# Ternary feed-forward of a fused transformer kernel: TensorE takes the down-projection after the up-projection, VectorE the residual after the gating, and ScalarE normalises into two buffers ahead of the silu

## What is computed

```python
def act_quant(x):
    scale = 127.0 / jnp.clip(jnp.max(jnp.abs(x), axis=-1, keepdims=True), EPS)
    return jnp.clip(jnp.round(x * scale), -128.0, 127.0) / scale
def weight_quant(w):
    scale = 1.0 / jnp.clip(jnp.mean(jnp.abs(w)), EPS)
    return jnp.clip(jnp.round(w * scale), -1.0, 1.0) / scale
def bitlinear(x, w):
    return jnp.einsum('bsd,hd->bsh', act_quant(x), weight_quant(w))
h = jax.nn.silu(bitlinear(x, w1)) * bitlinear(x, w3)
return bitlinear(h, w2)

x = x + ffn(layernorm(x), w1, w2, w3)
```

## Time and profile before

| | |
|---|---|
| median of 3 runs | 1206.63 us (1204.51 to 1207.88) |
| the profiled execution's own time | 1209.69 us |
| its span, first to last instruction | 1207.9 us |
| mean granted TensorE clock | 0.958 of full speed |
| busy over the span: TensorE, VectorE, ScalarE, GpSimd | 90%, 69%, 39%, 37% |
| the stage `bit_ffn` in it | from 246 to 402 us |

### The profile page before, as it was taken

The page is one execution under the profiler, slowest core; times in us unless marked ns, Lnnn a source line. Parts: engine busy times, 40 slices in busy tenths (PEclk is TensorE's granted clock), DMA queues, the critical chain, the costliest instruction groups (busy, mean ns, idle before and its releaser), DMA issues. The chain is left out here.

```text
span 1207.9 us, 21482 instructions
## 1 busy us (share of the span) xinstructions
PE 1086.0 (90%) x5900; PEld 811.4 (67%) x5912; DVE 829.0 (69%) x1572; ACT 475.1 (39%) x1008; POOL 442.6 (37%) x355
## 2 busy tenths in 40 slices
PE   6999799958988698999899987999999999999997
PEld 5989676523443357989887765777777776777773
DVE  3548447848887546877896985767677676666656
ACT  1332134235553148888521162333333333333330
POOL 0000001135442110577662002655556566565520
PEclk8999999979999698999888998999999999999998
DMA  7334251323233368556065314879788798777659
GB/s 264 139 122 165 101 195 23 71 47 66 55 59 57 101 228 306 203 190 228 1 250 198 62 53 161 221 181 243 189 234 228 189 248 232 186 189 180 137 112 360
DMA packets 148189, 195.48 MB, mean 162 GB/s; under 512 B 62986, under 2 KB 80778, under 8 KB 148145
## 3 DMA queue, kind: packets, MB, share of 16 engines
q1 hardware_dynamic: 130512, 156.61, 40.8%
q0 software_dynamic: 17632, 38.32, 16.0%
HBM read 136.56 MB, written 50.34 MB: 155 GB/s over the span
## 5 line engine op out<-in xcount | busy, mean ns | idle before, releaser
L2362 POOL DMA_INDIRECT y_d<-tail,x_ox x78 | 163.1, 2092 | 136.2 <-ACT tail L2589 105.5
L1647 POOL DMA_INDIRECT e_rows<-r_d,x_ix x80 | 85.3, 1066 | 123.6 <-issue 106.2
L2434 PE MATMUL x_h<-x_w_hi,x_t_hi 128*128 x320 | 127.7, 399 | 2.2 <-DVE x_t_lo L2603 2.2
L2435 PE MATMUL x_h<-x_w_lo,x_t_hi 128*128 x320 | 127.5, 399 | 0.0
L2436 PE MATMUL x_h<-x_w_hi,x_t_lo 128*128 x320 | 127.4, 398 | 0.0
L2603 DVE TENSOR_TENSOR x_w_lo<-w,x_w_hi (+1 forms) x64 | 109.6, 1752 | 2.6 <-ACT x_w_hi L2560 2.6
L2551 ACT ACTIVATE e_rows<-x_h 128x256 f32<-128x256 f32 x80 | 30.8, 385 | 183.7 <-PE x_h L2436 172.6
L213 POOL TENSOR_TENSOR ln_rstd<-ln_ve,powers 128x2 f32<-128x2 f32 (+1 forms) x40 | 34.2, 856 | 172.1 <-DVE ln_ve L207 172.0
L2603 DVE TENSOR_TENSOR x_t_lo<-x_xb,x_t_hi 128x512 fp32r<-128x512 f32 x80 | 55.2, 692 | 42.5 <-ACT x_t_hi L2546 35.2
L1527 DVE SCALAR_TENSOR_TENSOR h_c<-h_qk,h_d 128x768 f32<-128x768 f32 x64 | 58.2, 951 | 26.0 <-PE h_qk L1421 9.4
L2453 PE MATMUL x_o<-x_w_hi,x_avt_hi 128*128 x160 | 71.6, 448 | 1.2 <-issue 1.0
(11 more groups left out here) (408 smaller groups left out, 2596.2 us busy)
## 6 DMA issues: line engine op xcount, KB each, us to landing
w<-in_L_ffn_w SPq DMA_DIRECT2D x32, 1024.0 KB
w<-in_L_ffn_w SPq DMA_DIRECT2D x32, 512.0 KB
h_negm<-negm_d SPq DMA_DIRECT2D x15, 1024.0 KB, 7.0
raw<-in_L_ffn_w SPq DMA_DIRECT2D x3, 2816.0 KB, 16.9
x_res<-in_x SPq DMA_DIRECT2D x8, 512.0 KB, 4.4
ctx_in<-in_ctx SPq DMA_DIRECT2D x8, 512.0 KB, 3.5
kt_d<-ct SPq DMA_DIRECT2D x8, 512.0 KB, 2.7
vc_d<-ctx_in SPq DMA_DIRECT2D x8, 512.0 KB, 2.7
```

The lines of the kernel that those rows point to most:

```text
L1647: nc.gpsimd.indirect_dma_start(out=xg[q][s], out_offset=None, in_=r_d, in_offset=bass.IndirectOffsetOnAxis(ap=ix[q][:, s:s + 1], axis=0), ...
L2362: nc.gpsimd.indirect_dma_start(out=y_d[s], out_offset=bass.IndirectOffsetOnAxis(ap=ox[q][:, s:s + 1], axis=0), in_=eo[q][s][:], in_offset= ...
L2434: nc.tensor.matmul(hbank[s], hi[:, k, :], w13p[0][:, at, k, :], start=k == 0, stop=False)
L2435: nc.tensor.matmul(hbank[s], hi[:, k, :], w13p[1][:, at, k, :], start=False, stop=False)
```

## The change

1. TensorE: in a round, u of tile t comes before `down(t-2)`.
2. VectorE: in a round, `hidden(t)` comes before `residual(t-2)`.
3. `f_xn` becomes two buffers, taken in turn. `normal(t)` therefore waits for `integers_x(t-2)` in place of `integers_x(t-1)` (the count of `xq_ready`).
4. ScalarE: `normal(t+2)` comes before `silu(t)`.
5. Before the first round: ScalarE does `normal(0)`, `normal(1)`, `grid_x(0)`, `grid_x(1)`; VectorE and GpSimd do `moments(1)` ahead of `spread_x(0)` and `integers_x(0)`.

```diff
-    xn = sbuf(st, "f_xn", [P, D])
+    xn = [sbuf(st, f"f_xn{u}", [P, D]) for u in range(2)]
...
         moments(0)
+        moments(1)
         integers_x(0, 0, 0)
-        moments(1)
         scales(0, 0)
...
             up(par, g_bank, w1t, g_ps)
+            after(pe, u_used, t)
+            if first:
+                pe.wait_ge(turned.w3_in, 16 * turned.turns["w3"])
+            up(par, u_bank, w3t, u_ps)
             if inner or t >= 2:
                 if not inner and t == 2:
                     pe.wait_ge(turned.w2_in, 16 * turned.turns["w2"])
                 down(t - 2, par, m - 1)
-            after(pe, u_used, t)
-            if first:
-                pe.wait_ge(turned.w3_in, 16 * turned.turns["w3"])
-            up(par, u_bank, w3t, u_ps)
...
             act.wait_ge(nmr_ready, t + 1)
-            after(act, xq_ready, t)
-            nc.scalar.activation(xn[:], x[:, ds(t, 1), :].rearrange("p o d -> p (o d)"), ACT.Identity,
+            after(act, xq_ready, t - 1)
+            nc.scalar.activation(xn[par][:], x[:, ds(t, 1), :].rearrange("p o d -> p (o d)"), ACT.Identity,
...
+            if inner or t + 2 < NT:
+                normal(t + 2, par)
             silu(t, par)
-            if inner or t + 2 < NT:
-                normal(t + 2)
             if inner or t:
                 grid_h(t - 1)
...
-        normal(0)
-        grid_x(0)
-        normal(1)
-        grid_x(1)
+        normal(0, 0)
+        normal(1, 1)
+        grid_x(0, 0)
+        grid_x(1, 1)
...
+            hidden(t, par)
             if inner or t >= 2:
                 residual(t - 2, par)
-            hidden(t, par)
 
         moments(0)
+        moments(1)
         spread_x(0, 0)
-        moments(1)
         spread_x(1, 1)
```

More of the change, by code:

```diff
@@ L837, in integers_x @@
             pool.sem_inc(pool_tick, 1)
-            nc.gpsimd.tensor_scalar(xq[:, par], xn[:], ROUND, 127.0, ALU.subtract, ALU.min).then_inc(xq_ready, 1)
+            nc.gpsimd.tensor_scalar(xq[:, par], xn[par][:], ROUND, 127.0, ALU.subtract, ALU.min).then_inc(xq_ready, 1)
         def tile(t, par, m):
@@ L899, in _, with normal, grid_x @@
     def _(act):
-        def normal(t):
+        def normal(t, par):
             act.wait_ge(nmr_ready, t + 1)
-            after(act, xq_ready, t)
-            nc.scalar.activation(xn[:], x[:, ds(t, 1), :].rearrange("p o d -> p (o d)"), ACT.Identity,
+            after(act, xq_ready, t - 1)
+            nc.scalar.activation(xn[par][:], x[:, ds(t, 1), :].rearrange("p o d -> p (o d)"), ACT.Identity,
                                  bias=nmr[:], scale=norm.rstd[:, 0:1]).then_inc(xn_ready, 1)
-        def grid_x(t):
+        def grid_x(t, par):
             act.wait_ge(xs_ready, t + 1)
             act.wait_ge(xn_ready, t + 1)
-            nc.scalar.activation(xn[:], xn[:], ACT.Identity, bias=round_up[:], scale=scl[:]).then_inc(xa_ready, 1)
+            nc.scalar.activation(xn[par][:], xn[par][:], ACT.Identity, bias=round_up[:], scale=scl[:]).then_inc(xa_ready, 1)
         def grid_h(t):
@@ L930, in tile @@
             if inner or t + 2 < NT:
-                grid_x(t + 2)
+                grid_x(t + 2, par)
         act.wait_ge(round_ready, 2)
-        normal(0)
-        grid_x(0)
-        normal(1)
-        grid_x(1)
+        normal(0, 0)
+        normal(1, 1)
+        grid_x(0, 0)
+        grid_x(1, 1)
         tiles(act.Fori, tile, tile, tile)
@@ L961, in spread_x @@
             after(dve, xa_ready, t)
-            spread(xn, big, deq[:, par:par + 1], scl, xs_ready)
+            spread(xn[par], big, deq[:, par:par + 1], scl, xs_ready)
         def hidden(t, par):
```

## The result

| | before | changed |
|---|---|---|
| median of five runs each | 1206.37 us | 1197.36 us (1193.19 to 1199.29) |
| ratio, 95% interval | | 0.9913 (0.9888 to 0.9938) |
| the profiled execution's own time, and its span | 1209.69, 1207.9 us | 1199.29, 1197.5 us |
| the stage `bit_ffn`, from GpSimd's first memset to the end of the last residual | 155.1 us (246.93 to 401.99) | 145.2 us (247.12 to 392.33) |
| gating to gating, mean of the ten rounds from the third gating | 8.15 us | 7.71 us |

The change makes the kernel 9.0 us faster by the medians; 1195.2 us was forecast. In the profiled pair the span shrinks by 10.4 us, of which 9.85 lie in the stage.

What follows compares the result with a forecast made beforehand. A ring over three engines and the DMA bounds the kernel, VectorE next; ten rounds of 7.5 us, plus opening and last rounds, put the sixteenth gating 11.4 us earlier: 1206.63 - 11.4 = 1195.2 us, range 1193.0 to 1199.5.

Steps and rivals of the forecast that it cites:

- rounds of 7.65 us: Steady rounds, slow end of the range: 0.05 us at each of four waits on another engine; gain 9.9 us.
- a ring over three engines: Steady rounds before the change: TensorE, VectorE, ScalarE and the DMA delay one another, 8.05 us a round.
- both waits: Steady rounds before: TensorE's 10.1 us for `f_hqt` ahead of the down-projection, VectorE's 6.5 us for ScalarE's normalised row.
- The margin of 0.5 us: TensorE's down-projection behind u: transpose lands at H + 3.6, earliest start H + 4.1, H being a gating's start.
- I take 7.5 us a round: 7.42, and 0.08 for hand-overs that are now bare.: Steady rounds after the change: VectorE's packed 7.42 us plus hand-overs, ends 7.35 and 7.65, over ten rounds.
- Residual behind the gating: VectorE's rounds: moves 0.66 us behind the gating's scale, costs nothing, spares the gating a wait for `o_ps`.
- Normalising ahead of the silu: ScalarE's rounds: L904 from H + 1.0 to H + 1.8, silu loses nothing, VectorE's 6.5 us wait goes.
- The opening: Before the first tile: 1.8 us later for L838, first gating only 0.3 us later, 1.8 us won by the third.
- The last rounds: From the thirteenth gating L914's place decides: fifteenth after 12.9 us, sixteenth 7.14 later, then 15.6 us unchanged.
- No change: Rival: the ring closes again elsewhere, only the opening's 1.8 us come, 1204.8 us; chance 0.05.
- the serial ring: Rival: L914 behind the silu ties L952 to TensorE's g, 8.7 us a round, 1212.6 us; chance 0.05.
- GpSimd's lock on VectorE: Rival: GpSimd's L838 holds up VectorE's L948 in steady rounds, 3 us back, 1198.2 us; chance 0.10.

Runs made afterwards that it cites:

- the second trace: The changed kernel run again, unedited: 1197.61 us, ratio 0.9926, stage 144.8 us, rounds of 7.71 us.
- Two `f_hid` buffers: Changed kernel with the opening order of the kernel before, plus a second `f_hid` taken in turn: 1195.15 us, ratio 0.9886, stage 138.9 us.
- parts 1 and 2 alone: Kernel before with only down-projection behind u and residual behind the gating: one execution 1197.73 us, stage 144.9 us.
- The other two traces with the new opening: The changed kernel run again, 1197.61 us, and the changed kernel with the residual again ahead of the gating, one execution 1197.65 us.
- the old opening: Changed kernel with the opening put back in the order of the kernel before: 1194.89 us, ratio 0.988, stage 143.6 us.

## Why the prediction was right, and where it was not

- **The whole.** 1195.2 us forecast, 1197.36 measured, inside 1193.0 to 1199.5. The gain forecast was 11.4 us; the stage gave 9.9 (10.3 in the second trace). 9.9 is also the gain that I worked out for rounds of 7.65 us, and the rounds were longer; 0.6 us of it is luck, a last down-projection of 4.23 us where the kernel before had 4.87.
- **What bounds the kernel.** Right: a ring over three engines, and VectorE as the next bound. In the changed kernel both waits are gone and only VectorE is never idle for others. One step was read off by a round: the down-projection takes the transposed row of the L952 just before (L952 at 320.79, transpose issued 321.71, down-projection 325.34), and not "two rounds on" or from "a round and a half earlier". The margin of 0.5 us was worked out from H + 3.6, which has it right.
- **"I take 7.5 us a round: 7.42, and 0.08 for hand-overs that are now bare."** This term was mis-sized, and it is most of the miss: 7.71, so 0.29, outside the end of 7.65 that I gave. Ten rounds make 2.1 us. I had put it down to waits on other engines; it was a wait of VectorE on itself, in a step that I had costed at nothing.
- **"Residual behind the gating. Costs nothing, and spares the gating a wait."** The half that failed. I looked for what the residual might meet and not for what it had covered: it stood between L952 and the gating, which overwrites what L952 reads. Two `f_hid` buffers took 0.27 us off the round, which accounts for nearly all of the 0.29. At the end of the stage the same move pays: it takes the last three distances from 22.3 down to 20.15 us. In the steady rounds it about evens out, 7.71 us against 7.65 to 7.69 with the residual ahead, since there it also covers most of the loop's turn.
- **"Normalising ahead of the silu ... the 6.5 us go."** They go, but not by this: with parts 1 and 2 alone they are gone, since the silu mostly waits for the gating and no more for g. I had written that the two waits hang together and then given each part its own gain; the sum was safe from that, as it was made from the floor and not from the waits, but the credit was wrong. Its timing (L904 ending where the silu starts, margin of 2 us for L914) was exact, and so was the claim that with one buffer L904 waits until about 2.9 us after the gating (309.80 to 312.76) and L914 just keeps its time.
- **The opening.** 1.8 us were forecast for L838 of tile 0: it went from 252.39 to 254.50, with a start 0.19 us later, so 1.9. The first gating: 19.4 us after the start forecast, 19.63 and 18.56 measured; TensorE's clock decides between them. I had not seen that the table load now follows L904.
- **The last rounds.** 12.9 and 7.1 us forecast, 13.0 and 7.1 measured: L914 behind the silu behind g, as worked out. The 15.6 us behind the last gating came at 14.9 and 15.6.
- **The rivals.** No change and the serial ring did not come. Only the last rounds ran like the serial ring. GpSimd's lock on VectorE did not show either. In the steady rounds L838 ends 0.7 us before L948 starts (311.81 + 1.92 against 314.41), so they do not try it. But the opening of the changed kernel does:

```profile
254.42 0.69 DVE L947 TENSOR_REDUCE f_big<-f_xn 128x1 f32<-128x512 f32 x1 [1.81 <-ACT f_xn L910]
254.50 1.97 POOL L838 TENSOR_SCALAR f_xq<-f_xn 128x512 bf16<-128x512 f32 x1 [1.75 <-ACT f_xn L910]
255.14 0.15 DVE L948 TENSOR_SCALAR f_deq<-f_big 128x1 f32<-128x1 f32 x1
```

L948 starts 0.64 us into L838, which runs until 256.47, and 0.72 us behind its reduction, as it does everywhere; L203, at 256.11, is not held either. The other two traces with the new opening show the same. So L838 does not hold up the two operations that the rival named. Whether it would hold up a long one such as L952, no trace here shows. The other direction is in every trace: GpSimd's L213 takes 0.55 us alone and up to 1.3 beside L952.

What stays open: why the stages behind this one take 798 to 809 us from one execution to the next. No run here was made for that.

## What to carry to other kernels

When two engines wait for each other in a ring, count its cut once: make the sum from the next engine's packed time, and expect that any one of several cuts gives most of it in the steady rounds (0.45 and 0.33 of 0.45 us here). Before moving an operation on the bounding engine, ask what wait it covered by standing there (a buffer read by its forerunner, a loop's turn) and measure the distance start to start, not the durations. A second buffer pays where the bounding engine hands data over to itself, here on `f_hid`, and hardly where an engine with room waits, here on `f_xn`.

## What the runs showed of the hardware that I had not expected

- On VectorE an operation may start before the one in front has ended: 0.81 us start to start for L952, whose duration is 0.89. If it waits for that one's completion, it is 1.03 us.
- The turn of a hardware loop showed as 0.52 to 0.54 us of idle time on VectorE when a short one-column operation stood ahead of it. With a 0.75 us operation there it showed as 0.05, but that operation started 0.1 to 0.24 us later behind L949 inside the loop than outside. Where an engine waits at the turn anyway, the list of waits puts the turn down to that wait.
- One-column operations of VectorE (L948, L203) started at their usual distance while GpSimd's L838 was running; GpSimd's L213 took up to 1.3 us beside VectorE's L952 and 0.55 alone.
- TensorE's eleven matmuls of a down-projection took 2.54 us at full clock. The last one of the stage, for whose transpose it had stood 1.9 to 4.9 us, took 3.7 to 4.9 us in ten traces and 2.55 in two. Between the old opening and the two `f_hid` buffers that alone moves the stage by 1.4 us.
